# Interleaving the rows of the split Q and K operands in a two-layer attention kernel

## What is computed

```python
# layer 0
h = ln(x); q, k, v = h@sa_wq, h@sa_wk, h@sa_wv      # + biases, q * 16**-0.5
x = x + attn(rope(q), rope(k), v, causal=True) @ sa_wo
h = ln(x); q = h@ca_wq; k, v = ctx@ca_wk, ctx@ca_wv
x = x + attn(rope(q), rope(k), v, causal=False) @ ca_wo
x = x + gelu_tanh(ln(x) @ fc1_w) @ fc2_w
# layer 1
a = attn(x@Wq, ctx@Wk, ctx@Wv, causal=True) + x
h = ln(a)
out = gelu(h @ W1) @ W2 + h
# attn: s = einsum('blhd,bmhd->bhlm', q, k); p = softmax(s); einsum('bhlm,bmhd->blhd', p, v)
```

## Time and profile before

| | us |
|---|---|
| median of 3 runs | 1119.23 |
| lowest, highest | 1112.74, 1123.27 |
| span of the profiled execution | 1118.3 |

### The profile page before, as it was taken

The page is one execution under the profiler, slowest core; times in us unless marked ns, Lnnn a source line. Parts: engine busy times, 40 slices in busy tenths (PEclk is TensorE's granted clock), DMA queues, the critical chain, the costliest instruction groups (busy, mean ns, idle before and its releaser), DMA issues.

```text
span 1118.3 us, 13782 instructions
## 1 busy us (share of the span) xinstructions
PE 936.4 (84%) x5180; PEld 456.9 (41%) x5180; DVE 582.5 (52%) x1347; ACT 419.9 (38%) x822; POOL 73.3 (7%) x83
## 2 busy tenths in 40 slices
PE   3888864899988898888989867999887888987898
PEld 1433322345443353434445324633233454442365
DVE  5555637784667704488545675665125504415500
ACT  1133331342355625353422431167763323343421
POOL 2102000000000200000000001000000000000210
PEclk9988886799999999988999897999998999998999
DMA  7805462202132100645020401013004004022000
GB/s 275 102 1 73 75 139 43 24 2 27 23 38 30 29 1 20 94 51 66 1 30 1 57 13 17 10 40 48 1 20 57 2 1 57 2 37 22 1 19 19
DMA packets 47013, 43.85 MB, mean 39 GB/s; under 512 B 13510, under 2 KB 44386, under 8 KB 46434
## 3 DMA queue, kind: packets, MB, share of 16 engines
q1 hardware_dynamic: 46948, 42.98, 24.0%
HBM read 13.32 MB, written 2.10 MB: 14 GB/s over the span
## 4 chain that ended last, share of the span: by engine, by line
PE 57%; DVE 17%; DMA 10%; ACT 8%; SPq 5%; issue 4%; ACTq 0%; DVEq 0%
PE ps_exp L852 10%; PE ps_o L964 10%; PE ps_misc L835 10%; PE ps_max L889 8%; ACT probs L1200 5%; DVE mcol L1114 5%; SPq L695 4%; PE ps_exp L922 4%; DMA QA<-part 4%; PE ps_chain L814 3%; PE ps_chain L822 3%; DVE swap L1028 2%; DMA QC<-part 2%; PE ps_exp L927 2%; PE ps_chain L787 2%
## 5 line engine op out<-in xcount | busy, mean ns | idle before, releaser
L1114 DVE TENSOR_REDUCE mcol<-ps_max 128x3 f32<-128x462 f32 (+5 forms) x496 | 292.2, 626 | 181.9 <-PE ps_max L891 106.1
L1200 ACT ACTIVATE probs<-ps_exp 128x512 f32<-128x512 f32 (+3 forms) x544 | 261.1, 523 | 242.0 <-PE ps_exp L925 87.0
L889 PE MATMUL ps_max<-KA,QA 96*128 96x512 bf16 (+3 forms) x384 | 117.9, 359 | 55.3 <-DVE mcol L1114 24.4
L922 PE MATMUL ps_exp<-QA,KA 98*128 98x512 bf16 (+3 forms) x384 | 120.4, 350 | 26.1 <-ACT probs L1200 18.3
L835 PE MATMUL ps_misc<-hT,w_up 128*128 128x512 f32 x256 | 125.7, 615 | 7.2 <-ACT hid L1191 2.2
L852 PE MATMUL ps_exp<-w_down,hid 128*128 128x256 f32 x512 | 128.2, 388 | 0.0
L1191 ACT ACTIVATE hid<-ps_misc,col 128x512 f32<-128x512 f32 x64 | 44.0, 687 | 200.4 <-PE ps_misc L835 200.4
L852 PEld LDWEIGHTS ps_exp<-w_down,hid 128*128 128x128 f32 x512 | 94.5, 190 | 29.7 <-issue 15.5
L1248 POOL TENSOR_TENSOR part<-rot,part 128x512 bf16<-128x512 f32 (+1 forms) x36 | 40.8, 1133 | 923.2 <-DVE part L1038 923.2
L889 PEld LDWEIGHTS ps_max<-KA,QA 96*128 96x128 bf16 x384 | 39.2, 104 | 123.1 <-DVE mcol L1114 63.6
L964 PE MATMUL ps_o<-probs,V 128*17 128x512 f32 (+3 forms) x768 | 85.1, 517 | 3.2 <-ACT probs L1200 2.3
(11 more groups left out here) (109 smaller groups left out, 986.6 us busy)
## 6 DMA issues: line engine op xcount, KB each, us to landing
QA<-part SPq DMA_DIRECT2D x72, 128.0 KB, 5.1
QC<-part SPq DMA_DIRECT2D x72, 128.0 KB, 5.2
KA<-part SPq DMA_DIRECT2D x48, 128.0 KB, 5.2
xb<-in_x SPq DMA_DIRECT2D x8, 512.0 KB, 6.1
out<-xb SPq DMA_DIRECT2D x4, 512.0 KB, 3.0
KC<-part SPq DMA_DIRECT2D x24, 77.0 KB, 3.1
w_up<-in_fc SPq DMA_DIRECT2D x1, 1024.0 KB, 7.0
w_down<-in_fc SPq DMA_DIRECT2D x1, 1024.0 KB, 8.2
```

Of the source, the lines that this page charges most:

```text
L889: mm = pe.matmul(dst, q, kk, start=True, stop=not causal)
L922: mm = pe.matmul(bank[:, q0:CH], KA[:, g // NT, hh, (g % NT) * P:(g % NT + 1) * P], QA[:, hh, q0:CH], start=True, stop=(r < 0))
L1114: dve.tensor_reduce(dst, src, AX.X, ALU.max).then_inc(s_max_done, 1)
L1200: act.activation(probs[:, n % 2, h, q0:CH], ps_exp[exp_nth[s] % 2][:, q0:CH], ACT.Exp).then_inc(s_exp_done, 1)
```

## The change

One line of the `place` and `ctxk` steps on SP: the rows that product g takes in the operands. Before, product g had the 16 neighbouring rows 16g to 16g+15. Now it has every sixth row: dimension d goes to row 6d+g. The rule holds for Q and K alike, so each row of the contraction still multiplies the same two numbers; only the order in which they are summed changes. Rows 96 and 97 stay. No instruction is added, removed or moved on any engine: the rows of all five instruction streams are the same in both kernels, and the DMAs have the same sizes.

```diff
@@ -683,7 +683,7 @@
                         for g in range(NPROD):
                             if which[g] != i:
                                 continue
-                            rows_g = slice(g * HD, (g + 1) * HD)
+                            rows_g = slice(g, SROW, NPROD)
                             hs = slice(f * HH, (f + 1) * HH)
                             if k == "ctxk":
                                 sp.dma_start(
```

## The result

| | median us | runs | ratio to before, 95% interval |
|---|---|---|---|
| before | 1117.7 | 4 | |
| every sixth row | 1079.4 (1071.7 to 1080.7) | 4 | 0.9638 (0.9593 to 0.9683) |
| the same, in two later comparisons | 1078.9; 1077.3 | 4; 6 | 0.9652 (0.9625 to 0.9680); 0.9604 (0.9576 to 0.9633) |

The change takes 38 to 46 us off, 3.5 to 4%, where 26 us (2.3%) were forecast. The direction and the mechanism of the placements were right and the size was too small: 1079.4 lies 14 us under the 1093 of the forecast. It is outside the 1081 to 1101 that the forecast covered, in the stretch given to rival 3 (chance 0.06), and inside the wide range of 1078 to 1112 by 1.4 us.

What follows compares the result with a forecast made beforehand. PE's work (84% busy) was taken as the bound, with about 182 us of idle recoverable. Gains at waits for placements summed to 30.1 us, less 4, leaving 26: 1119.2 to 1093 us; forecast range 1081 to 1101, eight-in-ten 1078 to 1112.

Steps and rivals of the forecast that it cites:

- rival 3: More than forecast: queue gone everywhere, ceiling of 30.1 us reached, clock and DVE waits 8 more; under 1081 us; chance 0.06.
- Rival 2: The destination rows are not what limits a placement, so the time stays at 1119 us; chance 0.07.
- rival 1: Placements land earlier but little reaches the end of the program: 11 us gained, 1108 us; chance 0.17.
- SP's issue at nothing: SP's issue of placements (L695): stepped destination costs nothing extra, still 0.60 us each; bounds 25 us growth, 4 us shrinkage.
- Rival 4: Slower: SP takes longer to issue stepped destinations, 7.4 us per 0.1 us; over 1124 us; chance 0.04.
- The landing: Placement issue to landing: 2.8 us taken, so a single burst's last landing comes 2.6 us earlier.
- At 168: PE's idle of 4.28 us and DVE's 13.14 us wait for the reload of x: 2.6 us gained.
- at 477: PE's 5.14 us wait for a QA placement at 477.02: 4.0 us gained, DVE's norm being late next.
- at 676: PE's 13.00 us wait at 676.75: about 1.2 us gained of 2.6, since DVE's norm ends just after.
- At 858: PE's 6.47 us wait at 858.44: 2.6 us gained.
- The small waits: PE's five small QA waits (6.1 us) and four for QC (5.1): 11.2 us gained, a third (4 us) taken off.
- the granted clock: PE's clock, 0.50 after several idles: fewer or shorter idles may gain a few us; left out of the sum.

Runs made afterwards that it cites:

- experiments 1 to 3: Changed kernel with every second row of 32 (1073.9 us), then every third of 48 (1080.2 us); then a separate kernel timing only DMA bursts by destination rows.
- Experiment 4: Kernel before the change, plus matmuls of no use ahead of PE's waits at four places: 1109.7 us, ratio 0.9912.
- experiment 6: Every sixth row for only half the placements, against the kernel before: self-attention's only 1089.5 us; context's K and cross attentions' Q only 1102.9 us.
- experiment 5: Changed kernel plus matmuls of no use in PE's idles: three places 1077.4 us, six places 1075.2 us; six on top of every second row 1075.9 us.

## Why the prediction was nearly right in its parts and too small in its sum

- **What limits a placement: right.** Sixteen neighbouring destination rows, not reading, not pieces, not SP. Windows and landings of the changed kernel show it, and experiments 1 to 3 exclude the reach and the distance. Rival 2 (the destination is not the limit) falls, and rival 1 (little reaches the end) with it: it had 11 us. One argument on the way was weaker than it looked: K of the context (`KC`) was called in as a placement that isn't held up, but it too goes to sixteen neighbours, and its landing fell from 3.1 to 2.2 us. At 79 KB every 0.64 us, 123 GB/s, it only asked for about as much as these rows took.
- **SP's issue at nothing: right.** Median 0.600 us against 0.601; the longest one is 1.09 instead of 0.94. Rival 4 falls.
- **The landing: right in kind, 0.4 us too late.** 2.8 was taken, 2.4 came at the median; that is 2.7 us less than before, and 2.6 was used.
- **The sum over the waits: near, in part by luck.** Forecast 26 us less waiting, PE's idle time fell by 23.7. Some terms gave less than they were put at. On DVE the wait at 113.62 is gone, but of the 3.0 at L1035 2.5 are left, where 2.6 each were taken. At 168 the reload's wait on DVE fell from 13.14 to 11.66, 1.5 for 2.6, and PE's idle there from 4.28 to 2.71; the reload lands 8.2 us after its issue instead of 10.0. Others gave as much or more: the 3.3 at the start is gone; at 477 4.8 (5.14 to 0.35) for the 4.0 taken, and what is left is again the landing, not the norm named as late next; at 676 1.9 (13.00 to 9.87 + 1.21) for 1.2. At 858 it was 2.4 for 2.6. The small waits were 11.2 and all nine are gone from the list; the third that was taken off for others moving in was not seen as such. Naming what is late next paid at 676; the wait for `a_ctx` behind the one at 858 wasn't foreseen.
- **The step that failed: "Not counted: the granted clock ... a few us of gain."** It is 15.7 us of PE's busy time in the profiled pair, four tenths of the whole gain, and not a few. The profile before held it: a granted clock of 0.50 or 0.55 for some 10 us behind the longest waits, and a total of 158 us, 125 of them with PE at work, that I didn't add up. The one row that was read for it shows something else: in the window 159 to 160 PE is fully busy, and the nearest wait of the list, at 168.42, comes only after it. With the 15.7 in the sum, 26 + 16 = 42, the forecast would have been 1077. By the line through the changed kernel's own runs the same term is (0.949 - 0.925) x 800 = 19 us. Experiment 4 shows that the clock costs time apart from the waits: 7 to 13 us came back with the landings as late as before and the time outside PE's own work unchanged (182.1 and 181.9 us). Rival 3, the one that mentioned the clock, had 0.06; its time came, but not by its sum of a ceiling of 30.1 reached and 8 more.
- **Open:** how the clock's share divides over the places, and whether it adds up over them (experiment 6). The filled waits of experiment 5 show that it can't be had by keeping PE busy at will, and no run here separates what an idle costs afterwards by its length.

## What to carry to other kernels

When a DMA writes few partitions, look at which of them it writes: the same bytes to every second or sixth partition landed in 2.4 to 2.5 us where 16 neighbours took 5.1, and where the order of the rows is free, as in a contraction, that cost nothing here. When a change shortens waits of TensorE, price two things, the wait itself and the stretch at the lower clock that follows it, and read the second from the granted clock behind the longest waits before you forecast: PE's work at the lower level, not all time at it, is what counts. Beyond the point where nothing is queued (every third row, 3.0 us instead of 2.4) a still earlier landing gave no time that could be told with certainty.

## What the hardware showed that was not expected

- Rows 0 and 32 of a destination share a write path like rows 0 and 1 (13.15 and 13.40 us for four transfers of two rows of 32 KB; 2.6 us for most pieces), rows 0 and 64 don't (7.78; 1.2).
- The kernel got 7 to 13 us faster by 114 matmuls whose results nobody reads.
- The same program on the same chip differs by up to 12 us between runs (1067.8 at a mean clock of 0.961, 1079.8 at 0.949, every second row), and the granted clock goes with it; a difference of under 5 us between two layouts is still open after 10 and 14 runs.
